# Three attention and expert stages in one software pipeline: work moved between its slots, own tiles for one output, counting by sums

## The reference

```
x = x + attention_a(layernorm(x))   # 16 heads of 8, rotary, causal
x = x + experts(layernorm(x))
x = x + attention_b(layernorm(x))   # 16 heads of 8, other rotary angles, causal
x = x + experts(layernorm(x))
```

```
gl_v = (x @ Ws).reshape(b, t, h, e);  wv = topk_mask(gl_v, 2) * sigmoid(gl_v)
v = einsum('bthe,btek->bhtk', wv, einsum('btd,edk->btek', x, Wv))
attn = softmax(q * scale @ k^T) @ v          # no causal mask
mask_o = topk_mask((x @ Wd).reshape(b, t, h, e), 2)
out = einsum('bthe,bthk,ekd->btd', mask_o, attn, Wo)
```

## Time and profile before

| | us |
|---|---|
| median of 3 runs (2090.65 to 2092.62) | 2090.83 |
| the profiled execution, its own time | 2082.94 |
| its span, first to last instruction | 2081.2 |
| PE busy, matmul | 1704.4 |
| DVE busy | 1619.6 |
| ACT busy | 1260.7 |
| POOL busy | 1051.5 |

### The profile page before, as it was taken

One profiled execution on the slowest core, in us unless ns is written; L12 is line 12 of the kernel. 1 busy time (PEld: TensorE's weight loads), 2 busy tenths in 40 slices (PEclk: granted clock), 3 DMA queues, 4 the chain that ended last, 5 costly groups with the idle time before them and its releaser, 6 DMA issues.

```text
span 2081.2 us, 31948 instructions
## 1 busy us (share of the span) xinstructions
PE 1704.4 (82%) x10304; PEld 755.4 (36%) x10304; DVE 1619.6 (78%) x4088; ACT 1260.7 (61%) x2802; POOL 1051.5 (51%) x1124
## 2 busy tenths in 40 slices
PE   1557988889898888989888888989888898978775
PEld 0122433334343433434343433434333343434332
DVE  3647887888888888888889888888879888886451
ACT  0336758575675757566575757667585756657351
...
DMA packets 87364, 68.67 MB, mean 33 GB/s; under 512 B 10464, under 2 KB 82848, under 8 KB 87072
## 3 DMA queue, kind: packets, MB, share of 16 engines
...
## 4 chain that ended last, share of the span: by engine, by line
PE 48%; DVE 34%; ACT 9%; issue 4%; POOL 2%; SPq 1%; DMA 0%; POOLq 0%; DVEq 0%; PEld 0%; PEldq 0%; ACTq 0%
DVE ztmp L964 5%; PE Y L471 5%; PE S1c L406 5%; DVE nmaxF L853 4%; DVE S1a L847 4%; PE S2a L436 4%; ACT Pq L690 4%; DVE S1b L847 4%; PE Y L462 4%; ACT PT L675 4%; DVE S1c L847 3%; PE M L601 3%; PE S1b L406 3%; PE M L564 3%; PE S1a L406 3%
## 5 line engine op out<-in xcount | busy, mean ns | idle before, releaser
L1075 POOL TENSOR_TENSOR Z<-Z,ztmp 128x1280 f32<-128x1280 f32 x112 | 324.8, 2900 | 325.8 <-DVE ztmp L964 324.6
L1042 POOL TENSOR_SCALAR_AFFINE_SELECT PT<-PT 128x256 f32<-128x256 f32 (+1 forms) x640 | 252.5, 406 | 390.9 <-ACT PT L675 387.1
L1066 POOL TENSOR_TENSOR Vf<-Vf,ztmp 128x512 f32<-128x512 f32 x256 | 348.9, 1363 | 106.1 <-DVE ztmp L936 97.5
L675 ACT ACTIVATE PT<-S2a 128x512 f32<-128x512 f32 x320 | 191.1, 597 | 238.3 <-PE S2b L428 188.7
L679 ACT ACTIVATE PT<-S2a 128x512 f32<-128x512 f32 x256 | 153.5, 600 | 211.8 <-PE S2a L436 209.9
L471 PE MATMUL Y<-PT,Vf 128*64 128x512 f32 x1024 | 274.8, 617 | 0.0
L936 DVE TENSOR_TENSOR ztmp<-xv,wv_s 128x512 f32<-128x512 f32 x256 | 231.8, 905 | 2.8 <-POOL Z L1075 2.8
L847 DVE CUSTOM_DVE_ANT_0 S1b<-S1b,maskw 128x128 f32<-128x128 f32 (+3 forms) x368 | 174.9, 507 | 73.3 <-PE S1c L397 69.8
L406 PE MATMUL S1c<-Kf,Qf 64*128 64x512 f32 x352 | 207.9, 672 | 28.8 <-ACT Pq L690 26.6
L406 PE MATMUL S1a<-Kf,Qf 64*128 64x512 f32 x352 | 206.8, 668 | 20.7 <-ACT Pq L690 20.7
L462 PE MATMUL Y<-PT,Vs 128*9 128x512 f32 (+3 forms) x2048 | 194.8, 455 | 0.0
(11 more groups left out here) (100 smaller groups left out, 3536.9 us busy)
## 6 DMA issues: line engine op xcount, KB each, us to landing
Qs<-parts SPq DMA_DIRECT2D x192, 64.0 KB
Ks<-parts SPq DMA_DIRECT2D x192, 64.0 KB
...
```

The costliest lines, as they stand in the source:

```text
L675: nc.scalar.activation(PT[:, slot % 2, b, :], t[:, :], ACT.Exp, scale=SCALE_A).then_inc(exps_done.sem, 1)
L1042: last = nc.gpsimd.affine_select(out=v, in_=v, compare_op=ALU.is_ge, fill=0.0, base=0, pattern=pattern, channel_multiplier=-1)
L1066: nc.gpsimd.tensor_tensor(Vf[:, i, :, :], Vf[:, i, :, :], vtmp[:, n % VBUF, :, :], ALU.add).then_inc(v_acc.sem, 1)
L1075: nc.gpsimd.tensor_tensor(Z[:, :, :, :], Z[:, :, :, :], ztmp[:, hh % 2, :, :, :], ALU.add).then_inc(z_acc.sem, 1)
```

## The change

- The four projection pairs go to slots 6, 7, 0 and 1: `F_STEPS` becomes (6, 8), (7, 6), (0, 6), (1, 6). The last two belong to the next iteration.
- f_output goes from (2, 1) to (4, 1), on PE and DVE, with own tiles xrF and resF. ZT becomes a tile of its own. SP loads xrF at the start of the iteration and stores resF after the scatter of Qs and Ks.
- The experts' choice: comparisons at (7, 5) and (7, 6); the count as three sums (tensor_tensor, bfloat16, 640, 320 and 320 elements) at (7, 7), (7, 8), (7, 9); the sigmoid steps at (0, 2), (0, 5) and (0, 9) of the next iteration.
- The value products no longer use (1, 8) and (1, 9); slot 2 has six of them, at steps 0, 1, 3, 4, 6 and 8. Slots 3 to 5 are as they were.

More of the change, by code:

```diff
@@ L100, in attention_and_mixture @@
         xr = sb("xr", [P, NT, C])
+        xrF = sb("xrF", [P, NT, C])
         xn = sb("xn", [P, NT, C])
@@ L120, in attention_and_mixture @@
         res = sb("res", [P, NT, C])
+        resF = sb("resF", [P, NT, C])
         wqk_s = sb("wqk_s", [P, 2 * HF * DF])
@@ L153, in attention_and_mixture @@
         M0, M1 = pb("M0"), pb("M1")
-        M0_USES = ["rows1",
-                   "rows2", "ZT1", "F out",
+        M0_USES = ["rows1", "F k2",
+                   "rows2", "F k3", "ZT1",
                    "rows3", "A xnT", "A qp",
                    "A kp",
-                   "A yNT", "F xnT", "F gate1", "F gate3", "F k0", "F k1",
-                   "rows0", "F k2", "F k3"]
-        M1_USES = ["YT6",
-                   "YT7", "ZT0", "ZT2",
+                   "F out",
+                   "A yNT",
+                   "F xnT", "F gate1", "F gate3", "F k0",
+                   "rows0", "F k1"]
+        M1_USES = ["YT6", "F q2",
+                   "YT7", "F q3", "ZT0", "ZT2",
                    "YT0", "A q",
@@ L167, in attention_and_mixture @@
                    "YT3", "A v", "A out",
[L168 to L169 removed]
+                   "YT4", "F gate0", "F gate2", "F q0",
+                   "YT5", "F q1"]
         N_BANKS = [NA_B] * SA + [NF_B] * SF
@@ L388, in pass1 @@
                         pe.wait_ge(scattered.sem, scattered.at(j, 4 * NSP))
-                    if group == SA and b == 0:
-                        pe.wait_ge(*drained(j, "F q3", 1))
-                        pe.wait_ge(*drained(j, "F k3", 1))
+                    if group >= SA and b == 0:
+                        for use in (f"F q{group - SA}", f"F k{group - SA}"):
+                            pe.wait_ge(*drained(j, use, 1 if group - SA < 2 else 0))
                     pe.wait_ge(*s1_free(j, n + 1 - len(S1)))
@@ L557, in f_project @@
                     for i, use in enumerate((f"F q{p}", f"F k{p}")):
-                        if not f_prep:
+                        if not (f_prep if p < 2 else f):
                             skip(use)
@@ L742, in iteration @@
                             act.wait_ge(*filled(j, "A v", 1))
-                            act.wait_ge(*filled(j, "F k3", 1))
+                            act.wait_ge(*filled(j, "F k3"))
                             drain("A xnT", xnT[:, :], bank("A xnT")[:, :])
@@ L752, in iteration @@
                             drain("F xnT", xnT[:, :], bank("F xnT")[:, :])
-                        if at in F_STEPS and f_prep:
+                        if at in F_STEPS and (f_prep if at[0] > 5 else f):
                             f_copies(F_STEPS.index(at))
@@ L902, in f_compare @@
                         last.then_inc(pick_chain.sem, 1)
-                def f_count(half):
-                    dve.wait_ge(pick_chain.sem, pick_chain.at(j, 1, 1))
-                    n = E * NT * HF
-                    by = beaten_by[:, :, :, :].rearrange("p e t g -> p (e t g)")
-                    beats = cmp_[:, :, :, :].rearrange("p b a g -> p (a g) b")
-                    with nc.allow_low_precision(reason="counts of at most 4 are exact in bfloat16"):
-                        nc.vector.tensor_reduce(by[:, n * half:n * half + n], beats[:, n * half:n * half + n, :],
-                                                AX.X, ALU.add).then_inc(pick_chain.sem, 1)
+                def f_count(step):
[7 more added lines that the diff above has]
+                                                cmp_[:, 1 if step == 1 else 4, :, :], ALU.add).then_inc(pick_chain.sem, 1)
                 def f_sigmoid(step):
@@ L973, in f_output @@
                     dve.wait_ge(xrF_loaded.sem, xrF_loaded.at(j, 1, 3))
-                    dve.wait_ge(resA_stored.sem, resA_stored.at(j, 1, 2))
+                    dve.wait_ge(resF_stored.sem, resF_stored.at(j, 1, 4))
                     dve.wait_ge(*filled(j, "F out"))
-                    nc.vector.tensor_tensor(res[:, :, :].rearrange("p t c -> p (t c)"), bank("F out")[:, :],
-                                            xr[:, :, :].rearrange("p t c -> p (t c)"), ALU.add).then_inc(resF_ready.sem, 1)
+                    nc.vector.tensor_tensor(resF[:, :, :].rearrange("p t c -> p (t c)"), bank("F out")[:, :],
+                                            xrF[:, :, :].rearrange("p t c -> p (t c)"), ALU.add).then_inc(resF_ready.sem, 1)
                     dve.wait_ge(resF_ready.sem, resF_ready.at(j, 1, 3))
```

27 lines of the change are left out of this document (11 added, 16 removed).

## The result

The kernel after took 2097.6 us (2094.4 to 2100.7), beside 2089.9 for the kernel before in the same runs: ratio 1.0037, 95% interval 1.0025 to 1.0049. It is slower by 0.37%, where 3.5% was forecast.

The account below looks back on a forecast made before the run. No engine fills the span; the limit is an order of waits. Terms -2.0 + 4.35 + 2.4 - 3.4 + 3.9 = +5.25 us an iteration, x 14 = +73.5, on 2082.9, plus 7.9: 2164 us; range 2078 to 2190.

Parts of the forecast that it names:

- The sign: Whole kernel: slower, given a chance of 0.7, against faster 0.2 and no change 0.1.
- The step that failed: Slot 0: the sigmoid's +1 comes 2.15 us after the product's start, under POOL's Z sum (1.57 to 4.47), and is held.
- the terms +2.3 and +2.4 of slot 0: Slot 0: +2.3 us for the sigmoid's +1 held behind POOL's sum, +2.4 for the full clock rate lost after PE's wait.
- rival (b): Slot 0: late mask of step 2, DVE reaches the +1 before POOL's sum, no clock loss; +0.55 x 14, 2099; chance 0.1.
- Slots 6 and 7: DVE's saved work and PE's moved projections give -3.6 us, the comparisons' hold takes 1.6: together -2.0 an iteration.
- the 1.54: Slots 6 and 7: time in us that DVE gains for the three bf16 sums, taken from rows of comparisons.
- the comparisons' hold: Slot 7: the comparisons, reading two SBUF tiles, stand until POOL's sum into Z ends at 4.47: +1.6 us.
- Slot 0: Projection 2 on PE and the sigmoid steps and selection on DVE make it +2.05 us longer, before hold and clock.
- Slots 1 and 2: Projection 3 costs +1.55, full rate gives back 0.75, f_output's leaving 4.2: -3.4 us, bounds -4.5 and -0.9.
- the case that I had put at 1.7 more: Slots 1 and 2: the upper bound, -0.9 us, with projection 3 running at half rate.
- Slot 4: f_output's 24 passes enter where PE is nearly full; some 0.2 of 4.14 us absorbed: +3.9, bounds +2.8 and +4.2.
- Start and end: The first and last iterations, thinly filled, were left at 0.

Follow-up runs that it names:

- values_back: The kernel after with the value products at their old steps (first two at steps 8 and 9 of slot 1): 2101.7 us, ratio 1.0089.
- p2_early: The kernel after with projection 2 at step 8 of slot 7 and projection 3 at step 6 of slot 0: 2124.8 us, ratio 1.0171.
- proj_back: The kernel after with all four projection pairs back at (6, 8), (6, 9), (7, 6) and (7, 8): 2164.2 us, ratio 1.0352.
- compare_late: The kernel after with the comparisons at steps 7 and 8 of slot 7 and all three sums at step 9: 2173.7 us, ratio 1.0429.
- proj_back_early1: proj_back with the sigmoid's +1 at step 1 of slot 0 instead of step 2: 2117.7 us, ratio 1.0162.
- fout_sums: The kernel before plus the three sums, own tiles, output products in slot 4 and first two value products in slot 2: 2080.8 us, ratio 0.9970.
- choice_free: The kernel after with comparisons, sums and sigmoid at old places, second and third sum at step 0 of slot 7: 2119.2 us, ratio 1.0156.

## Why the prediction was wrong

The sign was right; the size was off by 66 us, 4.7 an iteration.

**The step that failed** is "So the +1 of the sigmoid (L917, now after step 2) comes 1.40 + 0.75 = 2.15 us after the product's start, and POOL's Z sum began at 1.57 and lasts to 4.47", and with it the terms +2.3 and +2.4 of slot 0. The +1 came at 2.29; the Z sum came at 2.82, and the +1 took 0.24 us. POOL does its masks in order ahead of the sum, and the mask of step 2 was late. I had this case as rival (b), with the row that speaks for it, and gave it 0.1 on the ground that "PE and ACT run ahead of DVE in the new slot 0". They didn't: PE stood 2.30 us for DVE at the end of slot 7, fell to half rate, and ran its first products of slot 0 late.

I had looked for the loss of the clock only behind the hold, in slot 0; it came one wait earlier and kept the hold away. The half rate is what counts, not the wait: in values_back PE waits as long and keeps the full rate in two iterations, and in these alone the sum comes at 1.57 and the +1 is held. p2_early gives PE work in that wait; PE keeps the full rate, the sum comes at 1.57, and the +1 is held 2.44 us in 14 of 16 iterations. The margin is small: in the kernel after the sum came 0.16 to 0.68 us behind the start of the +1. Rival (b) named the late mask but not the half rate, so that it came true is partly luck.

**Its price** I had as 2.3 + 2.4 = 4.7 us with the clock behind it. The five pairs with and without the hold (two of them in slot 7) give 22, 40, 42, 43 and 69 us, over 14 iterations 1.6 to 4.9 an iteration; the 2.44 us record and the 3.76 us wait of PE in proj_back are near the 2.3 and 3.9 forecast. The mechanism holds; it wasn't in the kernel after. Rival (b)'s 2099 is near the measured 2097.6, but by errors that cancel: it has +0.55 an iteration, where +1.8 was measured, and nothing for start and end, where -8.7 was.

**Slots 6 and 7**: -2.0 said, -4.3 measured. The three sums took 0.89 us, each from its start to that of the next record, not 1.54: the 1.54 came from float32 comparisons, and the bf16 rate that the Trainium skill gives (VectorE: DVE Perf Modes, "The perf-mode tier table") was right: 640 values took 0.48 us and 320 took 0.32, so 0.0005 us a value, half of the 0.00102 of the comparisons. That is 0.65. The other 1.6 is the comparisons' hold: it occurred as forecast (median 1.64 us, 15 of 16) but lay on no path: slot 7 keeps its 14.0 us without it (compare_late), and PE is busy for 13.66 of the 14.00 us. That the comparisons "stand until 1.57 + 2.90 = 4.47: +1.6" was read off one engine; what DVE would otherwise have waited for, projection 1, I didn't subtract. The rule of exclusive ports (the Trainium skill, SBUF — State Buffer, "SBUF: two separate sides") agrees with the rows shown here: a comparison 1.94 us against 0.22, TENSOR_SCALAR 2.94 against 0.23.

**Slot 0** without the hold: +2.05 said, +3.2 measured, with 3.41 us at half rate in each slot 0, which the sum had only behind a hold, and partly slot 7's work ending later: slots 7 and 0 together are 1.1 us shorter where -2.0 + 2.05 was said. What the 3.41 us cost there, no run shows. The 0.8 of idleness before the pair for step 8 is there (0.77).

**Slots 1 and 2**: -3.4 said, -1.8 measured, inside the bounds. Slot 2 gave 4.15 for 4.2. Slot 1 grew by 2.35: the full rate was not there, and projection 3 ran at half, the case that I had put at 1.7 more.

**Slot 4**: +3.9 said, +3.8 measured. **Slot 3**: nothing said, +0.9 measured; values_back shows it is the value products' steps. **Start and end**: 0 said, -8.7 in all.

Why each move alone costs 39 to 40 us is shown slot by slot only in part; the stretches at half rate, which lie differently in each kernel, may be the rest: in proj_back_early1 they are 12.1 us an iteration against 7.35 in fout_sums, but in choice_free only 6.6. I can't derive them, and that cause stays open.
